# Attention on one core: the third piece of each step issued ahead of the weighted values

## The reference, cut to what matters

```python
qkv = einsum('bsi,oi->bso', h, w_qkv) + b_qkv        # 16 heads, 16 channels each
attn = softmax(einsum('bhqd,bhkd->bhqk', q, k) / sqrt(16))
vals = einsum('bhqk,bhkd->bhqd', attn, v)
x = x + ga * (vals @ w_o.T + b_o)
h = layernorm(x) * (1 + cb) + sb
x = x + gb * (experts(h, top 6 of 32, chosen in 4 of 8 groups) + shared(h))
```

## Time and profile before

| | us |
|---|---|
| median of three runs | 1400.64 (1399.13 to 1400.97) |
| the profiled execution's own time | 1401.21 |
| its span in the profile | 1399.5 |
| TensorE busy | 1341.7 (96%) |
| VectorE busy | 1124.4 (80%) |
| ScalarE busy | 737.6 (53%) |
| GpSimd busy | 607.6 (43%) |

### The profile page before, as it was taken

One profiled execution on the slowest core, in us unless ns is written; L12 is line 12 of the kernel. 1 busy time (PEld: TensorE's weight loads), 2 busy tenths in 40 slices (PEclk: granted clock), 3 DMA queues, 4 the chain that ended last, 5 costly groups with the idle time before them and its releaser, 6 DMA issues.

```text
span 1399.5 us, 30567 instructions
## 1 busy us (share of the span) xinstructions
PE 1341.7 (96%) x8199; PEld 673.0 (48%) x8200; DVE 1124.4 (80%) x2816; ACT 737.6 (53%) x1127; POOL 607.6 (43%) x791
## 2 busy tenths in 40 slices
PE   6999999999999999999999999999999999999995
PEld 4562222333323323333233233668788888887542
DVE  6879999999999999999999992665566666666488
ACT  3551777767676767676767777123333333333100
POOL 1300122514634536445346366347755555555300
PEclk9996999999999999999999999999999999999998
DMA  6778665337446534463465446857766656656698
GB/s 201 227 231 199 139 166 114 66 77 162 86 110 142 127 89 107 119 163 84 101 152 150 91 127 213 252 171 229 227 200 198 201 170 188 181 166 181 243 339 338
DMA packets 264906, 235.31 MB, mean 168 GB/s; under 512 B 159286, under 2 KB 230470, under 8 KB 264684
## 3 DMA queue, kind: packets, MB, share of 16 engines
q1 hardware_dynamic: 237452, 159.23, 44.3%
q0 software_dynamic: 21872, 68.07, 13.8%
q10 hardware_dynamic: 5488, 6.82, 1.5%
HBM read 129.78 MB, written 104.22 MB: 167 GB/s over the span
## 4 chain that ended last, share of the span: by engine, by line
PE 71%; DVE 14%; DMA 3%; issue 2%; ACT 1%; POOL 1%; SPq 0%; DVEq 0%; POOLq 0%
PE psO L1250 15%; PE psE L1237 13%; PE ex_psGU L1758 13%; PE psM L1227 10%; DVE piece_max L1124 9%; PE ex_psY L1773 7%; PE ex_psX L1747 3%; PE psM L578 2%; DMA wide<-results 2%; PE ex_psA L1767 2%; PE psGU L1571 1%; PE co_psS L2027 1%; PE psM L597 1%; DVE wide L1988 1%; PE psX L1585 1%
## 5 line engine op out<-in xcount | busy, mean ns | idle before, releaser
L1124 DVE TENSOR_REDUCE piece_max<-psM 128x1 f32<-128x512 f32 x1024 | 642.6, 682 | 24.5 <-PE psM L1227 21.3
L1191 ACT ACTIVATE wide<-psE 128x1024 f32<-128x1024 f32 x512 | 497.2, 1021 | 203.4 <-PE psE L1237 201.1
L1227 PE MATMUL psM<-wide 48*128 48x512 bf16 x1024 | 323.5, 394 | 14.5 <-DVE piece_max L1124 12.5
L1237 PE MATMUL psE<-wide 49*128 49x512 bf16 (+1 forms) x2048 | 329.3, 380 | 0.3
L1839 POOL DMA_INDIRECT results<-vals_inv,places x223 | 214.0, 960 | 153.8 <-DVE vals_inv L1825 91.0
L1250 PE MATMUL psO<-wide 128*32 128x512 f32 x2048 | 273.9, 607 | 0.6 <-ACT wide L1191 0.6
L1227 PEld LDWEIGHTS psM<-wide 48*128 48x128 bf16 x1024 | 78.0, 93 | 342.7 <-DVE piece_max L1124 278.4
L1758 PE MATMUL ex_psGU<-wide,ex_xT 128*128 x892 | 232.3, 383 | 0.9 <-ACT ex_xT L1790 0.6
L1237 PEld LDWEIGHTS psE<-wide 49*128 49x128 bf16 (+1 forms) x2048 | 117.7, 95 | 89.2 <-issue 8.5
L1758 PEld LDWEIGHTS ex_psGU<-wide,ex_xT 128*128 128x128 f32 x892 | 152.0, 190 | 17.4 <-issue 4.4
L1790 ACT ACTIVATE ex_xT<-ex_psX 128x256 f32<-128x256 f32 x223 | 85.3, 383 | 121.7 <-PE ex_psX L1747 120.8
(11 more groups left out here) (280 smaller groups left out, 1234.2 us busy)
## 6 DMA issues: line engine op xcount, KB each, us to landing
wide<-qk_parts SPq DMA_DIRECT2D x384, 64.0 KB
wide<-results SPq DMA_DIRECT2D x16, 1536.0 KB, 9.4
rows<-lists SPq DMA_DIRECT2D x112, 160.0 KB
h2Ts<-lists SPq DMA_DIRECT2D x111, 160.0 KB
qk_parts<-parts SPq DMA_DIRECT2D x32, 384.0 KB, 2.9
xin<-in_x_dram SPq DMA_DIRECT2D x16, 512.0 KB, 4.1
wide<-in_guT_dram SPq DMA_DIRECT2D x3, 2560.0 KB
lists<-pad_row SPq DMA_DIRECT2D x32, 160.0 KB
```

Source lines behind the costliest of these rows:

```text
L1124: v.tensor_reduce(piece_max[:, qh, (x * PAIRS + h) * KT // QH + qt, kh:kh + 1], bank_of("piece", PIECES * group + n), AX.X, ALU.max, negat ...
L1191: nc.scalar.activation(probs[:, step % 2, 2 * pair:2 * pair + 2], psE[:, pair], ACT.Exp, scale=HD ** -0.5).then_inc(exp_ok, 1)
L1227: nc.tensor.matmul(bank_of(*user), qa[g][rows, h, qt * P:(qt + 1) * P], ka[g][rows, h, kh * 512:(kh + 1) * 512], start=True, stop=True).th ...
L1237: mm = nc.tensor.matmul(psE[:, pair, x], k[g][part, pair, kt * P:(kt + 1) * P], q[g][part, pair, qh * 512:(qh + 1) * 512], start=(q is qa) ...
```

## The change

In each step `piece(to, first + 2)`, P2, stands ahead of the weighted values O instead of behind them. P3 alone remains behind them. Nothing else is changed: the same instructions, the same waits, the same banks. The order in which the ring hands out its banks (P0, P1, P2, P3, R) is the same, and so are the orders of VectorE, ScalarE, GpSimd and SyncE.

```diff
@@ -1284,10 +1284,11 @@
                 scores(step, g, s, 1)
                 if to < NGR:
                     piece(to, first + 1)
+                if to < NGR:
+                    piece(to, first + 2)
                 if step:
                     weighted_values(step - 1)
                 if to < NGR:
-                    piece(to, first + 2)
                     piece(to, first + 3)
                 route_products(step)
             weighted_values(ALL - 1)
```

## The result

Timed 16 times each, the changed kernel takes 1403.88 us in the median, the kernel before 1401.43 (it was 1400.64 in the three runs shown ahead). The medians lie 2.45 us apart. The ratio taken from all the executions is 1.0023, with a 95% interval of 1.0013 to 1.0032: slower by 3.2 us, between 1.8 and 4.5. The profiled execution's span is 1402.1 us, against 1399.5.

A forecast was written before the change was run, and what follows sets the result against it. TensorE and VectorE, both nearly full, were taken as tied in a closed loop of 2.49 us a step. Plain steps add nothing; chunk terms of 0.84 sum to 5.7 us, a median of 1406.3, range 1401 to 1411.

The forecast's parts named there:

- Plain steps: Steps without a routing product: no change, still 2.49 us, with P3 taking P2's place in the same closed loop.
- The slot behind each R: Behind each routing product P2 needs a TensorE slot of its own: +0.22, against which a shorter wait of R can stand.
- The transposes: Step 21 of a chunk: VectorE's lead makes all 0.60 earlier, less the slot: -0.37 us; waits for P1 not beyond 0.3.
- The steps 13 to 15: Two statistics stand ahead of maxima, VectorE paces, and O waits for one maximum more: +0.68 us in all.
- The sign that was named: Around the chunk's step 14, an O to O of about 3.1 us where it was 2.49.
- Steps 24 to 31: Routing parts stand ahead of nearly each maximum and VectorE paces; one gap of 0.09 us more remains.
- The sum: All terms for a chunk: 0.84 us longer; six full chunks 5.0, the last 0.7, together 5.7 us.
- No price: Rival: the terms of R nearly cancel as VectorE's lead pays off elsewhere; 0 to 2.4 us, 1400.6 to 1403; chance 0.15.
- The open loop: Rival: plain steps fall to TensorE's own 2.42, some 150 of them; about 1396 us; chance 0.11 together with the 1394 rival.
- only the waits go: Rival: waits vanish and no slot costs anything, 7 us faster, 1394; chance 0.11 together with the rival at 1396.
- the price set on their failing: Rival: P3 and E0's first matmul share no slot, +0.15 in nearly all of 245 steps; 1434 us or more; chance 0.03.

The follow-up runs named there:

- The half maxima: Changed kernel and kernel before, each with maxima over 256 of 512 columns and scores scaled down by 16: 1348.31 us in the new order, 1343.92 in the old.
- the run without the four steps: The change in all steps but 11, 12, 22 and 23 of a chunk that hosts routing, against the kernel before: 0.9995 of its time.
- E0: Not a run: four matmuls behind P3 whose signal goes to ScalarE; with heads 1, 0, 1, 0 for 0, 1, 0, 1 in the changed kernel, 1405.34 us.

## Why the prediction was right, and where its size was off

**Plain steps.** Right as worked out: 2.49 before and after, P2 held at the place where P1 was, the loop's links 0.42, 0.69 and the O part unchanged. The run with four pieces ahead of O moves the one link that the loop says it should, and by its size.

**The slot behind each R.** Right: 4.59 to 4.64 (forecast +0.06, measured 0.05) and 4.44 to 4.64 (forecast +0.22, measured 0.20), 3.10 to 3.31, 4.41 to 4.62. The half maxima show it without VectorE, and its absence shows in the run without the four steps.

**The transposes.** Forecast -0.37, measured -0.34 in the chunk of the table (4.08 to 3.74), with -0.42 in others (4.15 to 3.73). The wait of the first transposes for P1 is 0.2, below the 0.3 that was named as the limit.

**The steps 13 to 15.** Here the sum was mis-sized. The mechanism came as described: VectorE's lead of one maximum is used up, and O waits for one maximum more (2.49 to 2.96, then 2.72 to 2.49). But of the two steps together 0.40 was forecast and 0.24 measured. My working has 1.05 from P1 to P2 and 0.95 from P2 to P3 (353.04, 354.09, 355.04). With a maximum of 0.60 that is 0.45 for the first statistic and 0.35 for the second, where the second one's row, 354.75 to 355.08, gives 0.33. The 0.55 from the first statistic to P2's maximum held 0.22 of waiting for P2, which started at 353.72 and is read 0.42 later at the earliest (354.14); the change takes this wait away. In the changed kernel P0 to P3 there take 2.46 (353.74 to 356.20), against 2.60 in my working: 0.14 of the 0.16. That is 0.16 in each of seven chunks, 1.1 us of the 1.3 between the 5.7 forecast and the 4.4 of the traces. The sign that was named, about 3.1 around step 14, came as 2.96.

**Steps 24 to 31.** Forecast +0.09. Measured from 25 to 30, the steps that change (2.85 + 3.33 + 3.70 + 3.98 + 2.96 + 2.49 against 2.58 + 3.40 + 3.70 + 4.04 + 2.77 + 2.76): 19.31 against 19.25, 0.06. Single steps move by up to 0.27 with both signs and cancel.

**The sum.** 0.84 for a chunk was forecast, 0.65 measured in the chunk of the table and 0.63 over the undisturbed chunks. From the 4.4 us of the traces to the 3.2 of the runs it is within the interval; the clock of the timed executions, which was lower in the kernel before, accounts for a part by the estimate above. In one thing the forecast had luck: 1403.88 lies just inside the 1403.5 to 1410 that had 0.68, and it does since the kernel before came out at 1401.43 and not at the 1400.64 that the forecast started from. Whether the change costs more than 2.8 us, which had 0.75, the timed runs leave open.

**The rivals.** "No price" (0 to 2.4 us): the interval, from 1.8, excludes no change but not the upper end of this rival. Against its mechanism stands the chunk, in which the terms don't cancel: five undisturbed ones are longer by 0.60 to 0.69 each. The open loop did not come: P2 stood at T + 1.17. That only the waits go is refuted by the slots. The pairs formed, and the price set on their failing rested on a queue that keeps its order, which the queue does not.

## What to carry to other kernels

Where a ring of buffers ties two engines, look for the closed loop: the first transfer behind the long block, its reader, the last transfer ahead of the block. Here, with a ring of three and four pieces a step, moving one piece across the block only renamed the links, and the wait that it removed came back one piece further on. What the move did change is how far the reader runs ahead, and that was paid or earned where the pace passes from one engine to the other, so it can be worth choosing step by step. And a duration is to be read from a row in which the engine did not wait.

## What the runs showed of the hardware

- Matmuls in the lower and upper 64 rows run side by side, and one of the free half starts ahead of up to two in the queue before it that need the other half. The signal kept the queue's order: ScalarE's exponential of E0 started 0.86 us behind P3 in both head orders (503.65 behind 502.80, and 503.99 behind 503.13, in single records of the traces), though in the second the matmul that carries the signal had started 0.21 us ahead of one that stands before it (503.36, 503.57).
- Each half takes one matmul of 512 columns in 0.22 us: with 8, 7 and 6 of them in the fuller half, a step took 2.84, 2.62 and, without the loop, 2.40.
- VectorE's end of a set of maxima (line 1131, which reads and writes arrays of 16 columns) took 0.18 us alone, and 1.33 to 1.37 beside GpSimd's operation of line 1007 in four chunks of the old order with half maxima, each time ending 0.03 us behind GpSimd's.
- The granted clock fell to 0.50, the lower of its two levels (1.2 GHz), for 3.4 us in step 28 of single chunks (492.2 to 495.6 us, before), which added 1.1 us to the run. It came again at step 28 in two of the other traces (the change in plain steps, and that in 13, 24 and 25, there in two chunks, and for 6.8 us in one of them, which cost 2.3 us), and at step 23 of two chunks in the run with the pieces of two steps in one half; in the rest of the traces it stayed at 1.00 from the second chunk to the last. What sets it off is open: in the kernel before TensorE was busy for the same 1.93, 1.57 and 1.77 us in the three stretches (2.0, 2.0 and 2.3 us long) ahead of this place in the fourth chunk, where the clock fell, and in the fifth, where it didn't.
